# A fused transformer layer in fp32: weights' operands in nine places, two tiles' operands in seven, and the operands' highs behind the scaling of the probabilities

## The reference

```
xn = layernorm(x)
qkv = xn @ w_qkv                      # 32 query heads, 8 key/value heads, 128 wide
attn = softmax(q k^T / sqrt(128) - slope_h * sqrt(i - j), causal)
a = (attn @ v) @ w_o                  # w_o: 4096 x 1024
f = xn @ W^T + b + lora(xn)           # one LoRA rank chosen per token by a gate
out = x + a + f
```

## Time and profile before

| | |
|---|---|
| median of three runs | 2513.1 us |
| lowest, highest | 2511.63, 2514.8 us |
| the profiled execution | 2510.83 us |
| its span in the profile | 2508.5 us |
| PE busy | 2413.6 us, 96% of the span |
| DVE, ACT, POOL busy | 60%, 55%, 31% |
| mean granted TensorE clock | 0.986 |

### The profile page before, as it was taken

The page is one execution under the profiler, slowest core; times in us unless marked ns, Lnnn a source line. Parts: engine busy times, 40 slices in busy tenths (PEclk is TensorE's granted clock), DMA queues, the critical chain, the costliest instruction groups (busy, mean ns, idle before and its releaser), DMA issues.

```text
span 2508.5 us, 35023 instructions
## 1 busy us (share of the span) xinstructions
PE 2413.6 (96%) x12128; PEld 2049.7 (82%) x12128; DVE 1503.8 (60%) x2817; ACT 1382.8 (55%) x3075; POOL 779.4 (31%) x1029
## 2 busy tenths in 40 slices
PE   5999999997899999999799999999999999999999
PEld 4787888886778888888688888888888888888887
DVE  6657455565755555545566666666656666666664
ACT  4432133334534123333777777777777777777764
POOL 3211000000320100000334535446345364454634
PEclk8999999998999999999999999999999999999999
DMA  4536344545345544543755565655656556555543
GB/s 148 189 132 213 134 161 158 201 174 218 115 135 185 176 151 168 201 169 141 279 193 188 184 214 182 219 175 182 220 188 218 185 183 212 195 201 201 185 168 126
DMA packets 118319, 455.93 MB, mean 182 GB/s; under 512 B 11945, under 2 KB 12089, under 8 KB 109184
## 3 DMA queue, kind: packets, MB, share of 16 engines
q1 hardware_dynamic: 86176, 334.37, 38.6%
q0 software_dynamic: 31968, 119.33, 13.7%
HBM read 276.96 MB, written 176.69 MB: 181 GB/s over the span
## 4 chain that ended last, share of the span: by engine, by line
PE 87%; ACT 5%; DVE 4%; DMA 2%; issue 1%; POOL 1%; SPq 0%; DVEq 0%; ACTq 0%; POOLq 0%
PE ps L637 27%; PE ps L639 27%; PE ps L638 27%; PE ps L824 5%; ACT wo L886 1%; ACT probs L1026 1%; DVE stats L1135 1%; ACT pt_hi L886 1%; DMA q<-qk_s 1%; ACT rows L915 1%; ACT probs L1040 1%; DVE w_lo L1121 0%; ACT res_hi L886 0%; DMA lora_lo<-lora_s 0%; DVE pt_lo L1121 0%
## 5 line engine op out<-in xcount | busy, mean ns | idle before, releaser
L886 ACT ACTIVATE w_hi<-raw 128x1024 fp32r<-128x1024 f32 x196 | 207.0, 1059 | 559.3 <-PE ps L639 440.3
L1121 DVE TENSOR_TENSOR w_lo<-raw,w_hi 128x1024 fp32r<-128x1024 f32 x196 | 239.1, 1224 | 357.8 <-ACT w_hi L886 357.6
L1389 DVE TENSOR_TENSOR acc<-ps,acc 128x512 f32<-128x512 f32 x448 | 298.3, 687 | 249.5 <-issue 225.1
L637 PE MATMUL ps<-x_hi,w_hi 128*128 128x512 f32 x1120 | 436.2, 389 | 0.0
L639 PE MATMUL ps<-x_hi,w_lo 128*128 128x512 f32 x1120 | 435.8, 389 | 0.0
L638 PE MATMUL ps<-x_lo,w_hi 128*128 128x512 f32 x1120 | 435.7, 389 | 0.0
L637 PE MATMUL ps<-wo,op_hi 128*128 128x512 f32 x896 | 365.5, 408 | 24.1 <-DVE wo L1121 24.1
L1026 ACT ACTIVATE probs<-probs,neg_max 128x512 f32<-128x512 f32 (+3 forms) x512 | 284.2, 567 | 172.2 <-DVE neg_max L1358 172.2
L639 PE MATMUL ps<-wo,op_lo 128*128 128x512 f32 x896 | 355.3, 397 | 0.0
L638 PE MATMUL ps<-wo,op_hi 128*128 128x512 f32 x896 | 354.4, 396 | 0.0
L1358 DVE CUSTOM_DVE_ANT_0 probs<-ps,bias 128x512 f32<-128x512 f32 (+3 forms) x512 | 220.7, 487 | 111.4 <-PE ps L639 107.5
(11 more groups left out here) (155 smaller groups left out, 4700.6 us busy)
## 6 DMA issues: line engine op xcount, KB each, us to landing
raw<-w_all SPq DMA_DIRECT2D x70, 1024.0 KB, 5.3
q<-qk_s SPq DMA_DIRECT2D x128, 512.0 KB, 3.9
acc<-acc_s SPq DMA_DIRECT2D x128, 512.0 KB, 5.2
acc_s<-acc SPq DMA_DIRECT2D x112, 512.0 KB, 7.8
qk_s<-res_hi POOLq DMA_DIRECT2D x40, 1024.0 KB, 4.6
qk_s<-res_a POOLq DMA_DIRECT2D x20, 1024.0 KB, 9.1
qk_s<-res_b POOLq DMA_DIRECT2D x20, 1024.0 KB, 5.2
k<-qk_s SPq DMA_DIRECT2D x32, 512.0 KB, 3.6
```

The costliest lines, as they stand in the source:

```text
L637: pe.matmul(to, st_hi, mv_hi, start=start, stop=False, skip_group_check=True)
L886: nc.scalar.activation(to, source, ACT.Copy).then_inc(signal, 1)
L1121: nc.vector.tensor_tensor(to, source, high.bitcast(F32), ALU.subtract).then_inc(signal, 1)
L1389: nc.vector.tensor_tensor(to, fill[f % 2][:, :], to, ALU.add).then_inc(s_acc, 1)
```

## The change

Three things change.

1. `wo` gets nine places that are used in rotation (`wo_place`), in the order `WO_TURNS`. A step's weights are then written over those of two turns back in the group before, and `used` names the product that must be over.
2. The heads' operands have seven places, one for each step: part p of a tile is written where part p - 7 stood, and each writer waits for that part's product (`op_used`). The sum of step 6 has a buffer of its own (`op_last`), since the place of step 6 is still in use then. The memory that this frees holds the two more places of `wo`.
3. The tables that set in which place of a group the weights' operands are made are rewritten, and in ACT's queue `normalise` stands ahead of the op highs.

```diff
-WO_SUMS_IN = {7: (4,), 8: (2, 3), 9: (5,)}
-WO_ORDER = (0, 1, 3, 2, 4, 6, 5)
...
+WO_SUMS_IN = {6: (4,), 8: (2, 3), 9: (5,)}
+WO_ORDER = (0, 1, 4, 3, 2, 6, 5)
...
-        wo = at("wo", 76 * K, [P, STEPS, 2, 1024], F32R)
-        op_hi = at("op_hi", 132 * K, [P, PARTS, 2, P], F32R)
-        op_lo = at("op_lo", 146 * K, [P, PARTS, 2, P], F32R)
+        wo = at("wo", 76 * K, [P, WO_PLACES, 2, 1024], F32R)
+        op_hi = at("op_hi", 148 * K, [P, STEPS, 2, P], F32R)
+        places = [(155 + i) * K for i in range(5)] + [54 * K, 55 * K]
+        op_lo = [at(f"op_lo{i}", place_, [P, 2, P], F32R) for i, place_ in enumerate(places)]
...
+        op_raw[6] = at("op_last", rest + 1664, [P, 2, P])
...
+        def op_used(s, part):
+            return PARTS * s + part - STEPS + 1
...
+        def wo_place(group, step):
+            return (STEPS * group + WO_TURNS.index(step)) % WO_PLACES
+
         def used(group, step):
-            return PARTS * (SETS // GROUPS * group - 1) + STEPS + step + 1
+            turn_ = STEPS * group + WO_TURNS.index(step) - WO_PLACES
+            if turn_ < 0:
+                return s_bank, 4 * TOTAL
+            last = SETS // GROUPS * (turn_ // STEPS + 1) - 1
+            return s_fill, PARTS * last + STEPS + WO_TURNS[turn_ % STEPS] + 1
...
             def out_high(s, part):
                 k = part % STEPS
-                if s:
-                    act.wait_ge(s_fill, PARTS * (s - 1) + part + 1)
+                if s or part >= STEPS:
+                    act.wait_ge(s_fill, op_used(s, part))
...
+                if n < UNITS:
+                    normalise(n)
                 for part in new:
                     out_high(s, part)
-                if n < UNITS:
-                    normalise(n)
                 for part in making(n, HIGHS_LAST):
                     out_split(*part)
```

More of the change, by code:

```diff
@@ L581, in out_sum @@
                 b11, b21, b12, b22 = at_blocks(s, tile)
-                to = op_raw[:, tile * STEPS + k]
-                first, second = {3: (b12, b11), 2: (b22, op_raw[:, tile * STEPS + 3]), 4: (b22, b12),
-                                 6: (b21, op_raw[:, tile * STEPS + 2])}[k]
-                if s:
-                    pool.wait_ge(s_fill, PARTS * (s - 1) + tile * STEPS + k + 1)
+                to = op_raw[k][:, :, :]
+                first, second = {3: (b12, b11), 2: (b22, op_raw[3][:, :, :]), 4: (b22, b12),
+                                 6: (b21, op_raw[2][:, :, :])}[k]
+                if k == 6 and (s or tile):
+                    pool.wait_ge(s_op_lo, op_used(s, tile * STEPS + k))
+                elif s or tile:
+                    pool.wait_ge(s_fill, op_used(s, tile * STEPS + k))
                 if k in (2, 6):
@@ L608, in wo_sums @@
                     pool.wait_ge(s_wo_raw[3], 16 * (group + 1))
[L609 to L612, removed]
+                if step in (2, 3):
+                    pool.wait_ge(*used(group, step))
                 if step != 4:
@@ L840, in fill_in @@
             def fill_in(s, tile, k):
-                part = tile * STEPS + k
-                f = PARTS * s + part
+                f = PARTS * s + tile * STEPS + k
+                home = wo_place(s // (SETS // GROUPS), k)
                 if s % (SETS // GROUPS) == 0 and tile == 0:
@@ L850, in fill_in @@
                     cols = slice(kt * 512, (kt + 1) * 512)
-                    last = product(fill[f % 2][:, :], (op_hi[:, part, kt, :], op_lo[:, part, kt, :]),
-                                   (wo[:, k, 0, cols], wo[:, k, 1, cols]), kt == 0 and k in STARTS, kt == 1)
+                    last = product(fill[f % 2][:, :], (op_hi[:, k, kt, :], op_lo[k][:, kt, :]),
+                                   (wo[:, home, 0, cols], wo[:, home, 1, cols]), kt == 0 and k in STARTS, kt == 1)
                 last.then_inc(s_fill, 1)
@@ L1051, in out_high @@
                     act.wait_ge(s_op_sum, len(OUT_SUMS) * s + OUT_SUMS.index((part // STEPS, k)) + 1)
-                high(op_hi[:, part], op_source(s, part), s_op_hi)
+                high(op_hi[:, k], op_source(s, part), s_op_hi)
             def out_split(group, step):
[L1056 to L1059, removed]
+                act.wait_ge(*used(group, step))
                 if step in WO_SUMS:
@@ L1064, in out_split @@
                     act.wait_ge(s_wo_raw[i], 16 * (group + 1))
-                high(wo[:, step, 0], wo_source(step), s_wo_hi)
+                high(wo[:, wo_place(group, step), 0], wo_source(group, step), s_wo_hi)
             deviation(0, 0)
@@ L1395, in out_split @@
                     dve.wait_ge(s_wo_sum, len(WO_SUMS) * (group + 1))
-                low(wo[:, step, 1], wo_source(step), wo[:, step, 0], s_wo_lo)
+                home = wo_place(group, step)
+                low(wo[:, home, 1], wo_source(group, step), wo[:, home, 0], s_wo_lo)
             deviation(0, 0)
```

35 lines of the change are left out of this document (18 added, 17 removed).

## The result

The kernel after takes 2526.1 us (median of five runs), the kernel before 2512.8 beside it: ratio 1.005, interval 1.0036 to 1.0063. It is slower by some 13 us, and lies 1 to 2 us beyond the range. (One of the five runs after took 13213 us, for a reason that is not known, and the ratio leaves it out; the other four lie between 2523.5 and 2527.6, their median is 2525.3.) The profiled execution took 2523.48 us with a span of 2521.5, so 13.0 us more of span than before.

What follows compares the result with a forecast made beforehand. PE, busy 96% of the span, was taken as the bound, so only its waits or lower clock could give time. Terms -1 + 1.5 - 4.5 + 3 = -1 gave 2510 us profiled, 2512.5 us median; range 2500 to 2524.

Steps and rivals of the forecast that it cites:

- rival 1: POOL's later op lows hold up DVE's weights' lows in each group, and with them PE; 2523 us, chance 0.17.
- Places 9 and 10: Chain through ACT and DVE to low 2: 0.1 us gained in each of seven groups, -1 us.
- The long piece: The longer of two pieces of PE's idle time in place 10, 2.3 to 2.5 us, beside one of 0.7.
- Places 7 and 8: Low 1 ahead of place 8's maxima makes `pt_lo` late, PE waits 0.1 to 0.2 us; +1.5 us, seven groups.
- Normal units: POOL's first op low comes 0.56 us later, within 0.65 us of cover after handing over; no change.
- seven places: Op operands: writers' waits for the product seven parts earlier end before they are reached; nothing.
- Clock: Place 10: half of seven clock drops, 1.4 us each, saved; -4.5 us, bounds 0 and -9.6.
- First group: Few PE parts, so added ACT and DVE work counts in full; +3 us, between +1 and +5.
- 4: Rival: POOL's first low is late in normal units, some 60 units; +15, 2528 us, chance 0.07.
- 5: Rival: the wait for low 2 keeps its size and clock; +4.5, 2517 us; counted within the forecast's 0.50.
- 2: Rival: ACT is on time in place 10, PE waits 1.6 us at full clock; 2495 us, chance 0.10.
- 3: Rival: the clock stays up in all groups, 4.5 to 5 us more than taken; 2508 us, chance 0.16.

Runs made afterwards that it cites:

- e6: The kernel after with three of the four quarters of POOL's sum for step 5 left out; 2518.4 us, ratio 1.0027.
- e5: The kernel after with low 4 moved behind the reciprocals and two additions in place 9; 2520.1 us, ratio 1.0029.
- e1: The kernel after with the op highs ahead of the scalings in ACT's queue, as before; 2503.3 us, ratio 0.9957.
- e7: The kernel after with low 1 early in place 8, ahead of the reciprocal, instead of last in place 7; 2527.3 us, ratio 1.0059.
- e3: Nine places for the weights and seven for the op operands, with the tables and ACT order of the kernel before; 2520.8 us, ratio 1.0025.
- e2: The kernel before with one edit, the scalings ahead of the op highs on ACT; 2529.2 us, ratio 1.0058.
- e4: As e3, with nine and seven places and before's tables, but with the scalings ahead of the op highs; 2536.7 us, ratio 1.009.
- v2: v1 with one edit, normalise ahead of the op highs again; 2482.7 us, ratio 0.9877.
- v1: The kernel after with op highs first, and turns, sums and tables changed so that lows 2 and 3 are made earlier; 2474.9 us, ratio 0.9851.

## Why the prediction was wrong

The forecast was no change, and the kernel is 13 us slower. The mechanism of rival 1, POOL beside DVE's weights' lows, made most of the miss; it was given 0.17, and its price of 2523 us, a median, is 3 us under the measured one, though partly by luck: it named low 1, low 3 and low 2, and measured are low 1 (1.45), low 4 (1.71) and low 2 (1.66), while low 3 took 1.25.

**Places 9 and 10: forecast -1, measured +7.8. This is the step that failed.** In us behind the start of place 9's scores (1558.21 before, 1563.66 after), the prediction's own chain:

| | before | predicted | after | miss |
|---|---|---|---|---|
| reciprocal | 7.24 | 7.24 | 7.73 | 0.49 |
| scalings | 7.87 | 7.45 | 7.93 | 0.48 |
| `pt_hi` | 14.65 | 14.51 | 15.02 | 0.51 |
| `pt_lo` | 15.27 | 15.13 | 15.63 | 0.50 |
| low 2 | 16.81 | 16.67 | 17.48 | 0.81 |
| PE's third part | 18.08 | 17.94 | 19.19 | 1.25 |

From the reciprocal to `pt_lo` the walk is right to 0.02 us; ACT's part of it holds. Each miss is where POOL comes in: 0.49 since low 4 took 1.71 ("1.15 us either way", said the prediction, by the row of low 0; but that low began when 0.14 us of a POOL operation were left, and low 4 when 0.63 were); 0.31 since low 2 waits for sum 5, which the prediction put at nothing; 0.44 since low 2 takes 1.66, not 1.21. The prediction had POOL 2 us later from the start and walked it only as far as the first part of place 10. It did not follow it to the sums that DVE waits for, nor set it beside the lows one by one. e6 shows the last two terms by taking away sum 5: 0.76 us. Low 4's term is read from the rows alone: e5, which takes it away, brings other waits at POOL in its place, so no run shows it by itself. e1 shows what the rest of the walk is worth: with the op highs ahead, the one high less brings `pt_hi` 0.95 us earlier than before, and PE's third part 0.92.

The wait for the first op low, forecast 0.7 with a long piece behind it, is there with 0.54; that it does not add to the chain is right too, as the table's last row is set by DVE. The long piece, forecast at 2.3 to 2.5, is 3.45.

**Places 7 and 8: forecast +1.5, measured +2.5.** The way is the one described: `pt_lo` is late for attn @ v. It lies 0.13 later than predicted, and low 1 took 1.45 beside POOL's op lows, 0.2 more than the walk gave it; e1 has 1.23 there and no wait. e7 shows that low 1 is the cause.

**Normal units and seven places.** Normal units are unchanged (949.1 us together before, 949.0 after): the cover of 0.65 held. "Seven places: nothing" came out true for the kernel after, but not for the reason given, that all these waits end before they are reached: with the old tables one of them, POOL's op sum behind place 10, lasts until PE's last part and costs 0.6 us per group (e3).

**Clock: forecast -4.5, measured -1.8.** Half of seven drops were to go; two went. In numbers, place 10 is +6.0 in all and its chain alone +7.8 (7 x 1.11, from the table's last row). The edge between waits of 2.33 and 2.49 us, which I read from two rows of the first group, does not exist: e1 has drops behind 2.19 and the kernel after has two waits of 3.45 without one.

**First group: forecast +3, measured +3.2, in part by luck.** The growth of the last wait past 3 us and the fall of the clock behind it are there (3.29 us). But by units, from place 5 to place 10, the differences are +1.7, -0.7, +0.3, +1.3, -2.4 and +3.1. The first is a clock drop behind waits of 1.64 and 1.78 us that are as long in the kernel before, where the clock stayed up. The wait that was to grow from 1.68 us to 3.5 is 1.76; the one a unit earlier grew instead, from 1.62 to 3.32. There low 0, made at the end of place 6, stands ahead of the maxima, and the prediction had put that low at nothing.

**The tail: not priced, measured +1.2.** At the very end, the last unit with parts has no other work to cover POOL's first op low:

```profile
2484.41 0.50 PE L656 MATMUL ps<-wo,op_hi 128*128 128x512 f32 x1 [0.95 <-POOL op_lo L616]
```

The same 1.2 us is in every kernel with the new order (e2, e4 to e7, v2), and in none without it.

Together -1 forecast and +13 measured; the miss of 14 is 8.8 in places 9 and 10, 2.7 in the clock, 1.2 in the tail, 1.0 in place 8 and 0.3 in all else. The rule of the Trainium skill that the prediction weighed and put at 0.17 ("SBUF — State Buffer", section "Who interferes with whom") is borne out in both directions: low 4, begun in the middle of POOL's sum 3, took 1.71 for 1.22, and POOL's two op lows at 1575.86, begun just behind low 3, took 2.42 for 1.42.

Of the other rivals, 4 (op lows late in normal units) and 5 (the wait untouched in size and clock) did not happen, nor did 2 and 3.

Still open is what decides whether the clock falls behind a wait in place 10. The chain fixes the wait (3.43 to 3.46 in all seven groups), and the drops differ from group to group and from kernel to kernel: with the same wait there is none in two groups and one of 1.5 us in five (after), and up to 2.7 us in e7. Some 3 to 7 us of the differences between these kernels are of that kind (an estimate: two drops of 1.5 us, up to the 6.9 us of e7), and no run sets it apart.

## What to carry to other kernels

When a step is moved, follow every engine that it makes late to the point where somebody waits for it, here POOL through a sum to DVE's low and PE, and give each element-wise operation the duration of a row that has the same neighbour on POOL, begun as long before the neighbour's end. Moving work ahead of what a slow engine needs shifts that engine's whole queue; the order cost 6 to 24 us here, though it cost nothing in normal units. Where a wait is at the end of a chain of four operations, making the last one a unit earlier can be worth more than shortening any of them (v1, 37 us, where the other steps' weights were moved as well).

## What the runs showed of the hardware

The length of PE's wait does not by itself decide on the clock. Waits of 3.44 to 3.46 us were followed by a granted clock of 0.50 in one group and of 1.00 in another of the same execution; waits of 3.11 had a drop in all seven groups of the kernel before; and in e1 a drop came behind five of seven waits of 2.19 to 2.21, and began 0.8 to 1.5 us after PE had started again, under full work. In the first group a wait of 1.78 us was followed by 0.50 in the kernel after and by no drop in the kernel before. A drop cost 1.3 to 1.6 us of a unit in most groups, and about twice that in some (e2, e3, e4, e7).

How long DVE and POOL hold each other up follows from when the later one begins. A subtraction on DVE of 128x1024 with both inputs in SBUF (a weights' low) took 1.19 to 1.24 us alone or where less than 0.15 us were left of a POOL operation. Otherwise it took longer by what was left of POOL's 128x256 operation (0.74), less 0.12. Low 2 of the kernel after had 0.58 left beside it and took 1.66, low 4 0.63 and 1.71, low 1 0.37 and 1.45, low 3 0.17 and 1.25; low 3 before 0.24 and 1.32. In the eleven traces this gives 615 of the 616 lows to within 0.04 us, the longest 1.79; the exception took 1.83 (e4). So a low lost no more than one POOL operation. The other way, a POOL operation of 128x256 took 0.73 alone, and 1.53 to 1.81 where it began with 0.9 to 1.2 us of a low left.
